# Layer 2 of a four-layer kernel: logits straight from x, and z by token beside the routing

## The chip, the cores and the metric

The kernel runs on one core of one Trainium2 chip. Times are device microseconds (us) of one execution. A core has a matrix engine (TensorE, PE in the views; PEld are its weight loads), a vector engine (VectorE, DVE), an activation engine (ScalarE, ACT), GpSimd (POOL) and a queue engine (SyncE, SP). Each runs its own list of instructions in order, and they wait for one another through semaphores. DMA queues move data between HBM and on-chip memory.

## What is computed

x is (2, 1024, 256), 2048 tokens of 256 numbers. Four layers add to it in turn. Each layer has a conditioning, z = cond(x), and a mixture of experts on z:

```
x = x + ffn0(cond0(x)); x = x + ffn1(cond1(x)); x = x + ffn2(cond2(x)); x = x + ffn3(cond3(x))
```

The change is in layer 2:

```
# cond2: one weight matrix (256 x 256) and one bias per batch row, by category
z = einsum('bti,bio->bto', x, W[cat]) + b[cat][:, None, :]
# ffn2
x_red  = z @ w_red                                  # 256 -> 16
wg_n   = wg / max(norm(wg, axis=1), 1e-4)           # 8 x 16
logits = x_red @ wg_n.T                             # 8 experts
gates  = softmax(logits); score = max(gates); idx = argmax(gates)
h = gelu(z @ W1[idx] + b1[idx])                     # 256 -> 512
o = (h @ W2[idx] + b2[idx]) * score                 # 512 -> 256
```

All of it is in fp32. Every large product is made of three matmuls: each operand is split into a high part (rounded to the engine's fast fp32r format) and a low part, and high x high, high x low and low x high are added up.

## The kernel before

Tokens lie on 128 partitions in NT = 16 tiles; NC = 4 chunks are 4 tiles each (512 tokens); KD = 2 is the number of 128-wide parts of the 256 features. The program is written out by hand: what an engine does next is the order of the code in its block, and semaphores (named `s_...`) tie the engines together. The change touches the seam between layer 1's expert blocks and layer 2's.

**Experts.** Layers 0 to 2 send each token to a block of 256 rows of its expert. `top1` (DVE) makes the softmax; `choose` in it marks the chosen expert; `ranks` (PE) counts tokens per expert with two fp32 matmuls; `order` (DVE) turns the counts into slots and writes one-hot tables (OHH, and OHL in four chunks); `slot_tokens` multiplies them on PE (16 matmuls), and on DVE turns the result into `slot_rows` (TOK), the list of token rows of each block. GpSimd then gathers rows of z from a copy in HBM (`z_rows`, ZD) by indirect DMAs into `w1_raw`, and `blocks` runs over pairs of blocks. GpSimd's first gather waits for slot_rows (`s_tok`) and for the stores of z (`s_zd`). SP's first two weight loads of a layer write over `z_tok` (Z), so that they too wait for `s_zd`.

**The seam before**, engine by engine, line numbers of the code before:
- SP: after layer 1's last block it reads y back from HBM into z_tok, chunk by chunk, then b[cat], spread over the partitions, into w2_raw (the last loop of `block_weights`).
- DVE: splits the conditioning's weights (`cond_split(2)`, L1728), adds y to x (`add_back`, L2050) and makes the low parts of x2's transposes (`lo`, L1717); then adds the bias to each tile of z (L2759), makes the low parts of z2's transposes, finishes the normalising of wg (L2763 to L2767), and starts `top1(2)`.
- PE: transposes x ("x2", L799) into featB; multiplies each token tile of x with W (6 matmuls, L787 to L789), which gives z by token; transposes z ("z2") into featA; multiplies with w_red (24 matmuls, 16 columns of weights); transposes wg_n (L1366); 16 fp32 matmuls for the logits (L1370); ranks(2), slot_tokens(2), blocks(2).
- ACT: the high parts of the transposes (L1389), a copy of x_red (L1694), the square root for the norm (L1696), the exponential (`exps`, L1401).

Layer 1 has no reduction, and takes its logits in another form, which `logits_t` and `logits` write: chunk by chunk the router (8 columns) is the stationary operand and the transposed z moves past it, ACT copies the 8 x 512 result, and 16 small transposes bring it back to tokens on partitions.

## Time and profile before

| | us |
|---|---|
| median of 3 runs | 1270.58 |
| lowest, highest | 1270.04, 1271.40 |
| profiled execution, as a run | 1275.55 |
| its span in the trace | 1273.9 |
| PE busy in the span | 1090.1 (86%) |
| DVE busy | 940.2 (74%) |
| ACT busy | 643.5 (51%) |
| POOL busy | 506.4 (40%) |

Durations in the rows come from the profiled execution, whose span is 1273.9 us; all times of day in the text are us from the span's start. "Idle before, releaser" in brackets behind a row is the time that the engine stood still ahead of it and what let it go; "issue" means that nothing visible held it. [...]

### The profile page before, as it was taken

Reading aid. Unit: us, or ns where it says so; the run is one execution under the profiler, and the core shown is the slowest. Engines: PE = TensorE matmul, PEld = TensorE weight load, DVE = VectorE, ACT = ScalarE, POOL = GpSimd, SP = SyncE. Lnnn points to the kernel's source line nnn. Section 1 sums busy time; section 2 is a strip of 40 time slices with the busy share of each in tenths; the row PEclk is TensorE's granted clock in tenths of the full one; section 3 lists DMA queues with packets and bytes.
Section 4 is the critical chain, followed back from the end, with each engine's and each line's share of the span. In section 5 each row is a group of like instructions: output and inputs, shape, how many; then the busy total and the mean of one; then the engine's idle time right before and its main releaser. Section 6 shows DMA issues by size and latency. Waiting matters only on the chain.

```text
span 1273.9 us, 25855 instructions
## 1 busy us (share of the span) xinstructions
PE 1090.1 (86%) x7884; PEld 1015.1 (80%) x7884; DVE 940.2 (74%) x1622; ACT 643.5 (51%) x1358; POOL 506.4 (40%) x345
## 2 busy tenths in 40 slices
PE   5788958999999999999968739997847976889796
PEld 4577958999999999999965539997737975668685
DVE  6767795888888888888837558884646866767695
ACT  3435316676676677677624537771225734313221
POOL 5000023878888888788730034542006760000000
PEclk8789888999999999999977859998758997989998
DMA  7300326677777778767540156653216844221202
GB/s 184 109 18 3 101 63 245 217 221 250 236 211 253 236 208 254 240 209 244 149 95 1 67 198 240 220 180 103 83 43 214 255 149 157 67 83 35 84 17 67
DMA packets 82030, 191.39 MB, mean 150 GB/s; under 512 B 16819, under 2 KB 57011, under 8 KB 69683
## 3 DMA queue, kind: packets, MB, share of 16 engines
q1 hardware_dynamic: 60050, 150.48, 34.8%
q0 software_dynamic: 21920, 40.21, 13.0%
q8 instruction: 26, 0.43, 0.1%
q14 instruction: 34, 0.27, 0.1%
HBM read 157.48 MB, written 33.18 MB: 150 GB/s over the span
## 4 chain that ended last, share of the span: by engine, by line
PE 68%; DVE 13%; issue 9%; DMA 5%; ACT 2%; DVEq 1%; SPq 1%; POOLq 0%; POOL 0%; ACTq 0%
PE ps L787 22%; PE ps L788 21%; PE ps L789 21%; PE ps L912 2%; DVE hidden_lo L1717 2%; PE ps L799 1%; DMA y_rows<-w_raw,slot_rows 1%; DMA w_raw<-z_rows,slot_rows 1%; DVE featB_lo L1717 1%; DVE x_tok L2050 1%; DVE featA_lo L1717 1%; DMA z_tok<-y_rows 1%; DVE w_lo L1717 1%; DMA z_tok<-in_L_w 1%; DVE z_tok L2446 0%
## 5 line engine op out<-in xcount | busy, mean ns | idle before, releaser
L1458 ACT ACTIVATE hidden_f<-ps,b_block 128x256 f32<-128x256 f32 x432 | 220.6, 511 | 172.4 <-PE ps L789 168.8
L677 POOL DMA_INDIRECT x_tok<-z_gate_rows,slot_rows x76 | 204.7, 2693 | 236.7 <-DVE slot_rows L1884 160.0
L1459 ACT ACTIVATE hidden_hi<-ps,b_block 128x256 fp32r<-128x256 f32 x432 | 222.4, 515 | 0.0
L1717 DVE TENSOR_TENSOR hidden_lo<-hidden_f,hidden_hi 128x512 fp32r<-128x512 f32 x284 | 183.9, 691 | 30.4 <-ACT hidden_hi L1459 16.0
L787 PE MATMUL ps<-w_hi,featA_hi 128*128 128x256 f32 (+1 forms) x624 | 179.4, 288 | 9.2 <-DVE featA_lo L1717 4.0
L787 PE MATMUL ps<-featB_hi,hidden_hi 128*128 128x256 f32 x616 | 175.9, 286 | 3.7 <-DVE hidden_lo L1717 3.7
L789 PE MATMUL ps<-w_hi,featA_lo 128*128 128x256 f32 (+1 forms) x624 | 178.9, 287 | 0.0
L788 PE MATMUL ps<-w_lo,featA_hi 128*128 128x256 f32 (+1 forms) x624 | 178.7, 286 | 0.0
L788 PE MATMUL ps<-featB_lo,hidden_hi 128*128 128x256 f32 x616 | 173.7, 282 | 0.0
L789 PE MATMUL ps<-featB_hi,hidden_lo 128*128 128x256 f32 x616 | 172.5, 280 | 0.0
L705 POOL DMA_INDIRECT x_rows<-w_raw,slot_rows x76 | 130.1, 1712 | 35.4 <-issue 21.9
L677 POOL DMA_INDIRECT w_raw<-z_rows,slot_rows x44 | 57.2, 1300 | 205.2 <-DVE slot_rows L1884 161.6
L787 PEld LDWEIGHTS ps<-w_hi,featA_hi 128*128 128x128 f32 (+1 forms) x624 | 122.0, 195 | 11.0 <-DVE featA_lo L1717 4.7
L788 PEld LDWEIGHTS ps<-w_lo,featA_hi 128*128 128x128 f32 (+1 forms) x624 | 121.8, 195 | 0.0
L789 PEld LDWEIGHTS ps<-w_hi,featA_lo 128*128 128x128 f32 (+1 forms) x624 | 121.8, 195 | 0.0
L787 PEld LDWEIGHTS ps<-featB_hi,hidden_hi 128*128 128x128 f32 x616 | 115.9, 188 | 4.3 <-DVE hidden_lo L1717 4.3
L789 PEld LDWEIGHTS ps<-featB_hi,hidden_lo 128*128 128x128 f32 x616 | 116.4, 189 | 0.0
L788 PEld LDWEIGHTS ps<-featB_lo,hidden_hi 128*128 128x128 f32 x616 | 115.8, 188 | 0.0
L1989 DVE TENSOR_TENSOR w_raw<-ps,b_block 128x256 f32<-128x256 f32 x120 | 49.7, 418 | 63.7 <-PE ps L789 58.0
L787 PE MATMUL ps<-w_hi,featB_hi 128*128 128x256 f32 x288 | 84.7, 294 | 8.7 <-DVE w_lo L1717 5.9
L1717 DVE TENSOR_TENSOR featA_lo<-scratch,featA_hi 128x2048 fp32r<-128x2048 f32 (+3 forms) x47 | 85.5, 1820 | 4.8 <-ACT featA_hi L1576 4.1
L787 PE MATMUL ps<-w_hi,hidden_hi 128*128 128x256 f32 x256 | 76.9, 301 | 8.2 <-DVE hidden_lo L1717 6.0
(446 smaller groups left out, 2969.6 us busy)
## 6 DMA issues: line engine op xcount, KB each, us to landing
scratch<-in_L_w SPq DMA_DIRECT2D x48, 1024.0 KB, 4.9
z_tok<-in_L_w SPq DMA_DIRECT2D x29, 1024.0 KB
x_tok<-in_L_w SPq DMA_DIRECT2D x19, 1024.0 KB, 4.9
b_block<-in_L_ffn_b POOLq DMA_DIRECT2D x60, 128.0 KB
...
```

Of the source, the lines that this page charges most:

```text
L677: gp.indirect_dma_start(XBL[L][:, k, tt, :], None, ZD if L else ZD0, bass.IndirectOffsetOnAxis(ap=TOK[:, q * BTT + tt:q * BTT + tt + 1], a ...
L705: gp.indirect_dma_start(XD, bass.IndirectOffsetOnAxis(ap=TOK[:, q * BTT + tt:q * BTT + tt + 1], axis=0), YB[:, k, tt, :], None, compute_op ...
L787: nc.tensor.matmul(out, lh, rh, start=first, stop=False)
L788: nc.tensor.matmul(out, lh, rl, start=False, stop=False)
L789: return nc.tensor.matmul(out, ll, rh, start=False, stop=last)
L799: last = nc.tensor.transpose(PS[:, g % 4, j * P:(j + 1) * P], src[:, c * TPC + j, k * P:(k + 1) * P], ident[:])
L912: last = nc.tensor.transpose(PS[:, 6 + k, m * BT + tt * P:m * BT + (tt + 1) * P], XBL[L][:, k, tt, m * P:(m + 1) * P], ident[:])
L1458: act.activation(HF[:, f // 2, part], ps, func, bias=b1)
L1459: act.activation(HTh[:, k, f // 2, part], ps, func, bias=b1).then_inc(s_hhi[L], 1)
L1717: return nc.vector.tensor_tensor(out, full, hi.bitcast(F32), ALU.subtract)
L1989: nc.vector.tensor_tensor(YB[:, k, j, :], PS[:, 4 + j, 0:D], B2B[:, k, :], ALU.add).then_inc(s_yev[L], 1)
L2050: nc.vector.scalar_tensor_tensor(X[:, n, :], Z[:, n, :], SM[:, 1, n:n + 1], X[:, n, :], ALU.mult, ALU.add).then_inc(s_add, 1)
```

## The change

With M = w_red @ wg_n.T (256 x 8), logits = (x @ W[cat] + b[cat]) @ M = x @ (W[cat] @ M) + b[cat] @ M. The changed kernel forms K = W[cat] @ M per batch row (256 x 8) and the constant b[cat] @ M, and takes the logits of layer 2 from the transposed x with K as router, in layer 1's form; z is no longer transposed.

- M is formed at the head of layer 1: the norm of wg (DVE, ACT's square root), a transpose and two small fp32 matmuls on PE, ahead of x1's transposes.
- K and the constant are formed between layer 1's blocks and x2's transposes: 8 + 4 fp32 matmuls on PE over the transposed W (WT2, two loads of 256 KB into hidden_f32 after layer 1's last hidden block) and the bias column CB2; DVE splits K and copies the constant.
- z keeps its matmuls by token. Its bias is now added on PE by two matmuls with one row each (a row of ones times the high and the low part of b), and ACT copies each tile to z_tok. Four tiles stand ahead of ranks(2), twelve behind it.
- The one-hot tables of layer 2 move from featB to featA, since featB still holds x.
- SP loads w_red and the bias transposed (the host prepares these and W transposed), two small loads more and one less at the kernel's start.

```diff
@@ SP, after layer 1's blocks
+                if L == 1:
+                    sp.wait_ge(s_hlo[1], steps * LAYERS[1][1] // P)
+                    for b in range(B):
+                        sp.dma_start(WT2[:, b], t["L2_cond_W_t"][bass.ds(cat[b], 1), :, :]
+                                     .rearrange("o (k p) i -> p (o k) i", p=P)).then_inc(s_craw, 16)
+                        sp.dma_start(BROW[:, b * D:(b + 1) * D], t["L2_cond_b"][bass.ds(cat[b], 1), :]).then_inc(s_craw, 16)
@@ PE, logits_t
+                if L in (1, 2):
+                    pe.wait_ge(s_tlo, TR0["z1" if L == 1 else "x2"] + KD * (c + 1))
+                if (L, c) == (2, 0):
+                    pe.wait_ge(s_reds, 3)
@@ PE, head of layer 1
+            pe.wait_ge(s_rstd, NT + 1)
+            nc.tensor.transpose(PS[0:GR, 7, 0:8], WG[:, 2 * GR:3 * GR], ident[0:8, 0:8]).then_inc(s_red, 1)
+            pe.wait_ge(s_reds, 1)
+            for k in range(KD):
+                last = nc.tensor.matmul(PS[:, 7, 16 + 8 * k:24 + 8 * k], WRT[:, k * P:(k + 1) * P], WGT[:], start=True, stop=True)
+            last.then_inc(s_red, 1)
             transposes("x1", X, lambda c: pe.wait_ge(s_x[c], 16 * 2))
@@ PE, the seam
-            transposes("x2", X, tiles_done(1))
-            pe.wait_ge(s_csplit, 3)
-            for n in range(NT):
...
-                last.then_inc(s_cy, 1)
-            transposes("z2", Z, lambda c: pe.wait_ge(s_z0, NT + TPC * (c + 1)))
-            pe.wait_ge(s_tlo, TR0["z2"] + KD * NC)
-
-            for c in range(NC):
-                for k in range(KD):
-                    last = mm3(PS[0:GR, c, :], Rh[2][:, k, :], Rl[2][:, k, :], TAh[:, k, c * CH:(c + 1) * CH],
-                               TAl[:, k, c * CH:(c + 1) * CH], k == 0, k == KD - 1)
-            last.then_inc(s_red, 1)
-            pe.wait_ge(s_rstd, NT + 1)
-            nc.tensor.transpose(PS[0:GR, 5, 0:8], WG[:, 2 * GR:3 * GR], ident[0:8, 0:8]).then_inc(s_red, 1)
-
-            pe.wait_ge(s_reds, 2)
-            for n in range(NT):
-                last = nc.tensor.matmul(PS[:, 4, n * 8:(n + 1) * 8], HF[0:GR, n // TPC, (n % TPC) * P:(n % TPC + 1) * P],
-                                        WGT[:], start=True, stop=True)
-            last.then_inc(s_lg, 1)
+            pe.wait_ge(s_reds, 2)
+            pe.wait_ge(s_craw, CRAW[2])
+            for b in range(B):
+                for m in range(KD):
+                    for k in range(KD):
+                        nc.tensor.matmul(PS[:, 7, m * 16 + b * 8:m * 16 + b * 8 + 8], WT2[:, b, k, m * P:(m + 1) * P], MCR[:, k, :],
+                                         start=k == 0, stop=k == KD - 1)
+                for k in range(KD):
+                    last = nc.tensor.matmul(PS[:, 7, 32 + b * 8:40 + b * 8], CB2[:, b, k:k + 1].broadcast_to([P, P]), MCR[:, k, :],
+                                            start=k == 0, stop=k == KD - 1)
+            last.then_inc(s_red, 1)
+
+            transposes("x2", X, tiles_done(1), lambda c: logits_t(2, c))
+            logits(2)
+
+            def z2(n):
...
+                if n >= 4:
                     pe.wait_ge(s_z0, NT + n - 3)
+                out = PS[:, n % 4, 0:D]
+                row = slice(b * D, (b + 1) * D)
+                nc.tensor.matmul(out, ONEh, BRh[:, row], start=True, stop=False)
+                nc.tensor.matmul(out, ONEh, BRl[:, row], start=False, stop=False)
                 for k in range(KD):
+                    w = slice((b * KD + k) * D, (b * KD + k + 1) * D)
+                    last = mm3(out, TBhv[:, k, n * P:(n + 1) * P], TBlv[:, k, n * P:(n + 1) * P],
+                               W1h[:, 1, w], W1l[:, 1, w], False, k == KD - 1)
                 last.then_inc(s_cy, 1)
+
+            pe.wait_ge(s_csplit, 3)
+            for n in range(TPC):
+                z2(n)
             ranks(2)
+            for n in range(TPC, NT):
+                z2(n)
             slot_tokens(2)
             blocks(2)
@@ ACT
-            transposes("x2", TBhv)
-            transposes("z2", TAh)
-            act.wait_ge(s_red, 1)
-            act.activation(HF[0:GR, :, :], PS[0:GR, 0:4, :], ACT.Copy).then_inc(s_reds, 1)
-            act.wait_ge(s_var, NC + 1)
-            act.activation(SM[0:8, 4, 0:1], SM[0:8, 4, 0:1], ACT.Sqrt).then_inc(s_std, 1)
+            transposes("x2", TBhv, lambda c: logits_t(2, c))
+            for n in range(NT):
+                act.wait_ge(s_cy, NT + n + 1)
+                act.activation(Z[:, n, :], PS[:, n % 4, 0:D], ACT.Copy).then_inc(s_z0, 1)
             exps(2, NT * 8)
@@ DVE, the seam
+            dve.wait_ge(s_craw, CRAW[2])
+            link(nc.vector.tensor_copy(BRh, BROW))
+            lo(BRl, BROW, BRh)
+            link(nc.vector.tensor_copy(ONEh, ONE[0:1, :]))
             cond_split(2, [(P, slice(0, B * KD * D))])
+            dve.wait_ge(s_red, 3)
+            km = PS[:, 7, 0:32].rearrange("p (k e) -> p k e", k=KD)
+            link(nc.vector.tensor_copy(Rh[2][:], km))
+            nc.vector.tensor_copy(CBL, PS[:, 7, 32:48].rearrange("p (b e) -> p b e", b=B))
+            link(lo(Rl[2][:], km, Rh[2][:]))
+            dve.sem_inc(s_reds, 1)
             add_back(1, "x2", TBhv, TBlv)
-            for n in range(NT):
-                dve.wait_ge(s_cy, NT + n + 1)
-                b = n // TPB
-                nc.vector.tensor_tensor(Z[:, n, :], PS[:, 4 + n % 4, 0:D], W2r[:, b * D:(b + 1) * D],
-                                        ALU.add).then_inc(s_z0, 1)
-            transposes("z2", TAh, TAl)
...
             top1(2)
```

PE, between the last matmul of layer 1's blocks and the first of layer 2's conditioning; before:

```order
L950 UNCONDITIONAL_BRANCH
L949 REGISTER_ALU
L949 COMPARE_AND_BRANCH
L799 MATMUL ps<-ident,x_tok 128x128 x32
L787 MATMUL ps<-w_hi,featB_hi 128x256
```

and now (router_raw holds M, hidden_f the transposed W, cond_b the bias column):

```order
L1377 MATMUL ps<-router_raw,hidden_f 128x8 x4
L1380 MATMUL ps<-router_raw,cond_b 128x8 x2
L1377 MATMUL ps<-router_raw,hidden_f 128x8 x4
L1380 MATMUL ps<-router_raw,cond_b 128x8 x2
L814 MATMUL ps<-ident,x_tok 128x128 x16
L802 MATMUL ps<-featB_hi,router_hi 8x512
L803 MATMUL ps<-featB_lo,router_hi 8x512
L804 MATMUL ps<-featB_hi,router_lo 8x512
```

Twelve small fp32 matmuls stand ahead of the transposes, and logits of a chunk follow the transposes of the next one.

PE, from z to the slot tables; before:

```order
L789 MATMUL ps<-featA_hi,router_lo 16x512
L1366 MATMUL ps<-ident,wg 16x8
L1370 MATMUL ps<-wg_t,hidden_f 128x8 x16
L888 MATMUL ps<-scratch,tri 128x128
L889 MATMUL ps<-scratch,ones 128x128
L897 MATMUL ps<-featB_lo,featB_hi 128x32 x16
```

and now, where four z tiles end and the other twelve begin (L1393 and L1394 are the one-row bias matmuls, L907 and L908 the ranks):

```order
L804 MATMUL ps<-w_hi,featB_lo 128x256
L907 MATMUL ps<-scratch,tri 128x128
L908 MATMUL ps<-scratch,ones 128x128
L1393 MATMUL ps<-w_hi 128x256
L1394 MATMUL ps<-w_lo,w_hi 128x256
L802 MATMUL ps<-w_hi,featB_hi 128x256
L803 MATMUL ps<-w_lo,featB_hi 128x256
```

The ranks stand between z tiles, and slot_tokens stands behind all sixteen of them.

DVE, ahead of layer 2's add; before:

```order
L2752 TENSOR_REDUCE small<-wg 8x1
L1728 CAST w_hi<-w_raw 128x1024
L1717 TENSOR_TENSOR w_lo<-w_raw,w_hi 128x1024
L2050 SCALAR_TENSOR_TENSOR x_tok<-z_tok,small,x_tok 128x256 x8
L1717 TENSOR_TENSOR featB_lo<-ps,featB_hi 128x512 x2
```

and now:

```order
L2798 CAST w_hi<-hidden_f 1x512
L1751 TENSOR_TENSOR w_lo<-hidden_f,w_hi 1x512
L2800 CAST w_hi<-ones 1x128
L1762 CAST w_hi<-w_raw 128x1024
L1751 TENSOR_TENSOR w_lo<-w_raw,w_hi 128x1024
L2804 CAST router_hi<-ps 128x32
L2805 COPY router_raw<-ps 128x2x8
L1751 TENSOR_TENSOR router_lo<-ps,router_hi 128x32
L2086 SCALAR_TENSOR_TENSOR x_tok<-z_tok,small,x_tok 128x256 x8
```

The split of the bias row stands ahead of the weights' split, and the three operations on PE's result stand between it and the add.

## Rows read from the trace of the kernel before

**Rows 1.** page, part 4: chain that ended last, by engine.

```profile
PE 68%; DVE 13%; issue 9%; DMA 5%; ACT 2%; DVEq 1%; SPq 1%; POOLq 0%; POOL 0%; ACTq 0%
```

**Rows 2.** stretches: us, busy of each engine (x instructions), granted clock, DMA.

```profile
890.50:903.00 12.50, 10.34 (x50) 9.53 (x51) 10.76 (x23) 4.78 (x8) 0.00 (x0) 0.54 0.24 76
...
912.40:937.50 25.10, 18.66 (x91) 12.88 (x89) 6.21 (x16) 8.96 (x12) 0.00 (x0) 0.77 0.07 24
```

**Rows 3.** chain of waits over the seam: start us, us, what.

```profile
913.02 2.90 DMA z_rows<-z_tok
...
961.14 0.58 PE L787 MATMUL ps<-w_hi,featB_hi 128*128 128x256 f32 x1 [1.41 <-issue]
```

**Rows 4.** timelines of POOL and PE: first gathers, layer 1's first block matmul.

```profile
748.30 1.02 POOL L677 DMA_INDIRECT w_raw<-z_rows,slot_rows  x1 [92.64 <-DVE slot_rows L1884]
...
952.23 0.99 POOL L677 DMA_INDIRECT w_raw<-z_rows,slot_rows  x1 [68.92 <-DVE slot_rows L1884]
...
758.79 0.58 PE L787 MATMUL ps<-w_hi,featB_hi 128*128 128x256 f32 x1 [1.41 <-DVE w_lo L1717]
```

**Rows 5.** timeline of PE: start us, us, engine line op, [idle before <-releaser].

```profile
930.37 6.99 PE L1370 MATMUL ps<-wg_t,hidden_f 16*128 16x8 f32 x32 [0.25 <-DVE wg_t L2767]
```

**Rows 6.** timeline of PE, layer 1: from 128 rows to 16.

```profile
717.04 0.29 PE L1308 MATMUL ps<-featB_hi,hidden_lo 128*128 128x258 f32 x1
717.25 0.38 PE L1314 MATMUL ps<-featA_hi 16*128 16x258 f32 x1
717.48 0.28 PE L1315 MATMUL ps<-featA_lo,featA_hi 16*128 16x258 f32 x1
717.60 0.28 PE L1316 MATMUL ps<-featA_hi,featA_lo 16*128 16x258 f32 x1
```

**Rows 7.** timelines at layer 1's end: PE's last matmul, then DVE.

```profile
881.33 0.28 PE L789 MATMUL ps<-featA_hi,hidden_lo 128*128 128x256 f32 x1
...
883.97 0.16 DVE L2751 TENSOR_TENSOR wg<-wg 8x16 f32<-8x16 f32 x1 [1.89 <-issue]
...
888.83 3.26 DVE L2050 SCALAR_TENSOR_TENSOR x_tok<-z_tok,small,x_tok 128x256 f32<-128x256 f32 x8 [2.65 <-DMA z_tok<-y_rows]
...
900.93 0.69 DVE L1717 TENSOR_TENSOR featB_lo<-ps,featB_hi 128x512 fp32r<-128x512 f32 x1 [0.16 <-ACT featB_hi L1389]
```

**Rows 8.** timelines of PE and ACT, head of layer 1.

```profile
662.01 5.87 PE L799 MATMUL ps<-ident,x_tok 128*128 128x128 f32 x32 [11.85 <-DMA x_tok<-x_rows]
...
669.30 0.69 ACT L1639 ACTIVATE hidden_f<-ps,cond_b 64x512 f32<-64x512 f32 x1 [0.65 <-PE ps L789]
```

**Rows 9.** timelines, layer 1: DVE's last low part, its softmax, ACT's z copies.

```profile
729.45 1.29 DVE L1717 TENSOR_TENSOR featA_lo<-ps,featA_hi 128x512 fp32r<-128x512 f32 x2 [0.97 <-ACT featA_hi L1389]
...
733.53 0.29 DVE L1755 TENSOR_TENSOR scratch<-ps,br 128x128 f32<-128x128 f32 x1 [2.51 <-PE ps L825]
...
719.41 1.57 ACT L1659 ACTIVATE z_tok<-ps,small 128x256 f32<-128x256 f32 x4 [1.72 <-DVE small L2712]
```

**Rows 10.** timeline of PE, layer 1: transposes of z and logits.

```profile
721.03 3.63 PE L799 MATMUL ps<-ident,z_tok 128*128 128x128 f32 x16 [2.07 <-ACT z_tok L1659]
...
724.96 0.40 PE L789 MATMUL ps<-featA_hi,router_lo 128*8 128x512 f32 x1
...
725.89 1.03 PE L799 MATMUL ps<-ident,z_tok 128*128 128x128 f32 x8
```

**Rows 11.** timelines of DVE and PE: routing of layer 2.

```profile
937.47 0.29 DVE L1757 COPY scratch<-ps 128x128 f32<-128x128 f32 x1 [6.86 <-PE ps L1370]
...
939.57 0.80 PE L888 MATMUL ps<-scratch,tri 128*128 128x128 f32 x2 [2.20 <-DVEq L1792]
...
940.82 0.29 DVE L1816 COPY scratch<-ps 128x128 f32<-128x128 f32 x1 [1.37 <-PE ps L889]
...
946.95 2.49 DVE L1845 TENSOR_TENSOR featB_hi<-lane,slot_low 128x512 fp32r<-128x512 int32 x4
...
947.69 3.59 PE L897 MATMUL ps<-featB_lo,featB_hi 128*128 128x32 f32 x16 [6.90 <-DVE featB_hi L1845]
```

More of the change, by code:

```diff
@@ L207, in build @@
         RHT = [[x[:, k, 3, 0:B * P] for x in (HTh, HTl)] for k in range(2)]
+        WRT = W1r[0:GR, 2 * P:2 * P + D]
+        MCR, CBL = Rr[2][:, :, 0:8], Rr[2][:, :, 8:16]
+        WT2 = HF[:, 0:2, :].rearrange("p b (k i) -> p b k i", k=KD)
+        BROW = HF[0:1, 2, :]
+        BRh, BRl, ONEh = W2h[0:1, 0, 0:B * D], W2l[0:1, 0, 0:B * D], W2h[0:1, 1, 0:P]
         CR0 = HF[:, 0:2, :].rearrange("p a c -> p (a c)")
@@ L234, in build @@
         s_craw = sem("cond_raw")
-        CRAW = [16 * n for n in (2 * B, 2 * B + 1, 3 * B + 1, 4 * B + 1)]
+        CRAW = [16 * n for n in (2 * B, 2 * B + 2, 5 * B + 2, 6 * B + 2)]
         s_csplit = sem("cond_split")
@@ L406, in _ @@
             sp.dma_start(B1[0][:], t["L0_b1_t"]).then_inc(s_cb0, 16)
-            for L, name in enumerate(("L0_ffn_Wr", "L1_ffn_Wr", "L2_ffn_w_red", "L3_router_t")):
+            for L, name in ((0, "L0_ffn_Wr"), (1, "L1_ffn_Wr"), (3, "L3_router_t")):
                 sp.dma_start(Rr[L][:], t[name].rearrange("(k p) e -> p k e", p=P)).then_inc(s_small, 16)
@@ L553, in block_weights @@
                                  ).then_inc(s_x[c], 16)
-                if L == 1:
-                    for b in range(B):
-                        sp.dma_start(W2r[:, b * D:(b + 1) * D], t["L2_cond_b"][bass.ds(cat[b], 1), :]
-                                     .broadcast_to([P, D])).then_inc(s_rows, 16)
             for L in SPARSE:
@@ L896, in slot_tokens @@
                         pe.wait_ge(s_inv, 15 + (1 + NC) * (L - 1) + n // TPC + 2)
-                    last = nc.tensor.matmul(PS[:, 5, 16 * NT:16 * NT + SCOLS[L]], OHL[:, n, :], OHH[:, n, :],
+                    last = nc.tensor.matmul(PS[:, 5, 16 * NT:16 * NT + SCOLS[L]], OHL[L][:, n, :], OHH[L][:, n, :],
                                             start=n == 0, stop=n == NT - 1)
@@ L1395, in logits_t @@
             def logits_t(L, c):
+                E = 8 if L == 2 else RW[L]
                 act.wait_ge(s_lt, LT0[L] + c + 1)
-                act.activation(LT[0:RW[L], c, :], PS[0:RW[L], 5 + c % 3, :], ACT.Copy).then_inc(s_lts, 1)
+                act.activation(LT[0:E, c, :], PS[0:E, 5 + c % 3, :], ACT.Copy).then_inc(s_lts, 1)
             def exps(L, n):
@@ L1633, in _ @@
             blocks(0)
+            act.wait_ge(s_var, NC + 1)
+            act.activation(SM[0:8, 4, 0:1], SM[0:8, 4, 0:1], ACT.Sqrt).then_inc(s_std, 1)
             transposes("x1", TAh)
@@ L1756, in softmax @@
                 else:
-                    link(nc.vector.tensor_copy(lg, ps))
+                    bte = "p (b t) e -> p b t e"
+                    link(nc.vector.tensor_tensor(lg.rearrange(bte, b=B), ps.rearrange(bte, b=B),
+                                                 CBL.unsqueeze(2).broadcast_to([P, B, TPB, E]), ALU.add))
                 link(nc.vector.tensor_reduce(SM[:, 5, :], lg, axis=AX.X, op=ALU.max))
@@ L2556, in _ @@
             next(masks)
-            for n in range(1, 4):
+            for n in (1, 3):
                 router_split(n)
```

58 lines of the change are left out of this document (31 added, 27 removed).

## The prediction

> **What bounds the kernel now.** The chain of waits comes first: PE holds 68% of it [rows 1], nearly all of that in the expert blocks. The change touches none of the expert blocks, only the seam between layer 1's last block and layer 2's first. So the second view is the table of stretches over that seam [rows 2]. [...] The seam is thus one serial chain: x added up and transposed, z made (903.0 to 912.4), z transposed, reduced and turned into logits (912.4 to 937.5, 25.1 us), routing (to 952), gather (to 961.1). Before the block can start, the list of rows (slot_rows) and the stored z rows must both be there. The chain shows that the last z tile's store runs from 913.02 to 915.9, after which nobody waits for a store; the gather starts at 952.23 and the block's first matmul at 961.14 [rows 3, 4]. Today routing is last, by 36 us. The reader should keep two clocks in mind below: when the rows are listed, and when z is stored.
>
> **Ahead of the add (+0.2 us).** PE gets 12 small fp32 matmuls in front of x2's transposes and DVE waits for them before its add. An fp32 matmul is two instructions in this trace (32 for the 16 of L1370), so 24. Their pace is bounded by two rows: L1370's 32 in 6.99 us at half clock (0.218 each), and 0.12 from start to start, the pace of full-clock matmuls [rows 5, 6]: 2.9 to 5.2 us. PE's last block matmul ends at 881.6; DVE needed 1.9 us to leave the same loop [rows 7], and I take the same for PE: 883.5 to between 886.4 and 888.7. DVE's own chain is 883.97, 1.3 us for the three bias splits, 2.0 for the weight split and some 0.7 for the three new copies: 888.0 to 889.4. The add starts at 888.83 today because y lands then [rows 7]. I take 889.0: +0.2, between 0 and +0.6. The transposed weights (512 KB) are loaded once the last hidden block is split, around 872, and have 11 us; nobody waits for them. The square root and the normalised gate weights move to the head of layer 1, where PE waits 11.9 us for x; I cost them nothing, but they leave another activation table loaded, and the reload (1.28 us) comes just before tanh, where ACT has 0.65 us free [rows 8]. That is +0.6, between 0 and 1.3.
>
> **Logits from x (32.9 us earlier).** Layer 1 already does what layer 2 now will: from its last featA_lo (ends 730.74) to softmax's first operation (733.53) are 2.8 us [rows 9]. Layer 2's last featB_lo ends at 901.6 [rows 7], +0.2 = 901.8, so softmax starts at 904.6 instead of 937.47. PE must keep pace for that. Per chunk it has six logit matmuls at 0.23 us and eight transposes in about 1.0 (four logit starts from 724.96 to 725.89, then 1.03) [rows 10], 2.4 us against DVE's 2.9 (four adds, two splits), at full clock. What goes away (z's 32 transposes, the 24 reductions, their copies, the Sqrt chain and the 7 us of L1370) needs no price, since the sum is built forward.
>
> **z on PE (the term that decides).** PE keeps its order: four z tiles, the rank matmuls, twelve z tiles, then slot_tokens. A tile is 6 matmuls at 0.12 us plus two with one row for the bias: 8 x 0.119 = 0.95. But the one-row pair needs the array with another number of rows. Where the trace switches from 128 rows to 16, the starts are 717.04, 717.25, 717.48, 717.60: two gaps of 0.21 and 0.23 where 0.12 is the pace, 0.20 lost for a switch [rows 6]. Each tile switches twice: 0.95 + 0.39 = 1.34 us; the bounds are 0.95 and 1.34, and I take 1.34, the nearest row. [...]
>
> Tiles 0 to 3: 904.4 + 5.4 = 909.8. Without them the ranks would start 2.1 us after softmax (939.57 against 937.47), at 906.7, so 3.1 us of the gain are given back. Ranks take 1.25 us at half clock [rows 11]; I take 0.7 at full clock. DVE's ordering then runs from 910.5 for 8.6 us (940.82 to 949.44) to 919.1 [rows 11]. PE's other twelve tiles: 910.4 + 12 x 1.34 = 926.5. PE, not DVE, is last, by 7.4 us. Two things follow from tile 15. slot_tokens: 16 matmuls, 1.9 us at full clock (3.59 at half [rows 11]), and DVE's three operations, 0.8: the rows are listed at 929.2. z: ACT's copy 0.45 (four in 1.57 in layer 1 [rows 9]), store 2.9 [rows 3]: 930.05. So **z's store becomes the last wait** in place of the list, and the gather starts at 930.3 instead of 952.23. ACT's exponential stands behind all 16 copies, with its table load: 928.8, just ahead of where DVE asks for it; nothing.
>
> **Gather and weights.** Gather to first matmul is 8.9 us in layer 2 (952.23 to 961.14) and 10.5 in layer 1 (748.30 to 758.79), where two weight loads of 1 MB follow the gather [rows 3, 4]. In the changed kernel the first-weight loads write over z and so also wait for the store: 4 x 512 KB leave with the gather, as many bytes as in layer 1. I take 10.5 (bounds 8.9 and 13). First block matmul: 940.8 against 961.14, a gain of 20.3; less 0.6 in layer 1, **19.7 us**. The clock that the block starts with (0.50) is the same, since PE idles some 10 us before it in both. From there on nothing moves. The profiled execution took 1275.55 us for a span of 1273.9; the span becomes 1254.2, and the median, 1270.58, becomes **1250.9, say 1251**.
>
> **Rivals.** [...] (B) PE runs the x2 stage at half clock. Today the stretch 890.5 to 903.0 stands at 0.54 [rows 2]. Layer 1's transposes begin at half clock too, and the clock is back after 3.4 us of unbroken work [rows 10]; here the first 16 transposes and the first logits join likewise, but later chunks leave gaps. At half clock a chunk takes 6 x 0.43 + 1.97 = 4.5 us against DVE's 2.9, some 5 us over the stage, up to 3 more on the first z tiles: 1256 to 1259, say 1257. (C) Gathers queue behind 2 MB of weights that today have long landed: 3 to 5 us more, 1255. (D) Slower than before: the engine falls to half clock in the stage and stays there as it did from 930 to 937, with PE busy throughout [rows 5]. The seam would still be 5 us shorter (z tiles 34 us instead of 21), but each us of block work costs another 0.8; from 6 us of blocks at half clock on beyond what they have now, the gain is gone, and 12 us of it give 1275. Against it: every block so far reaches 1.00 within 6 us. (E) The bias by PE makes DVE free, but z is not hidden beside routing, only partly: that is in the forecast, not apart.
>
> **How the numbers follow.** Forecast 0.52 (its own range 1247 to 1254: the store or gather some 3 us off), A 0.20, B 0.18, C 0.08, D 0.02. The predicted time is the likeliest case's, 1251. The range goes from A's 1243 to B's 1258 and leaves out less than 2 in 10. A measurement of this kernel tells about 0.2% (2.5 us) from no change: faster 0.96; same 0.02, for B and C together with a gather that is worse still; slower 0.02.
>
> **What would show it.** In the changed profile: softmax's first operation of layer 2 near 904.6 (B: 909 or later); starts of the z tiles 1.34 us apart (A: 0.95), with gaps at the one-row pair; slot_tokens following tile 15 at once, and DVE idle some 7 us before it; the gather released by the z store and not by slot_rows, near 930; first block matmul 10.5 us behind it. The forecast is wrong if the routing, and not z's store, is again last, if the add of layer 2 starts later than 889.5, or if the clock of the stretch from 895 to 926 is below 0.9.

## The result and the profile after

The changed kernel takes 1264.6 us (median of ten runs, 1254.5 to 1268.1) where the kernel before takes 1271.3 (ten runs, 1266.1 to 1274.6). The ratio is 0.9941, 95% interval 0.9916 to 0.9967: faster, but by 0.6% only. That is 6.7 us from median to median where 19.6 were forecast, and 6.6 us above the upper end of the range. The profiled execution has a span of 1264.9 us (before: 1273.9). Two executions far longer than the rest of their kernels (2701.4 us of the kernel before, 1295.8 us of the one below with pairs in tiles 0 to 7) are left out of all medians and ratios.

The chain that ended last has the same shape as [rows 1]. First the page of the changed kernel, part 4:

```profile
PE 68%; DVE 13%; DMA 7%; issue 6%; ACT 2%; POOL 1%; POOLq 1%; SPq 1%; DVEq 0%; ACTq 0%
```

The stretches of the changed kernel that answer to [rows 2] (us, busy time of PE, weight load, DVE, ACT, POOL with their instructions, granted clock, DMA share, GB/s):

```profile
886.90:894.00 7.10, 5.34 (x22) 4.05 (x23) 6.65 (x15) 2.39 (x4) 0.00 (x0) 0.54 0.59 189
894.00:901.50 7.50, 7.39 (x51) 4.06 (x50) 5.05 (x12) 4.29 (x8) 0.00 (x0) 1.00 0.00 0
901.50:904.30 2.80, 2.80 (x20) 2.40 (x18) 1.81 (x6) 0.38 (x1) 0.00 (x0) 0.90 0.03 6
904.30:909.00 4.70, 4.70 (x18) 3.80 (x18) 0.00 (x0) 0.77 (x2) 0.00 (x0) 0.50 0.00 0
...
930.00:937.00 7.00, 7.00 (x26) 5.66 (x26) 0.00 (x0) 1.15 (x3) 0.00 (x0) 0.50 0.21 70
```

Read the clock column, the number behind POOL's: the granted clock as a share of full clock, 1.00 full and 0.50 half. While x is transposed and the logits are made, the clock comes up to 1.00, at 893.5. In the z tiles it stands at 0.50 from 903.7 to their end at 937.5, 33.8 us in which PE is busy throughout. The timeline of PE shows where it fell (L1393 and L1394 are the one-row bias matmuls, L802 to L804 the products of full height; start, duration in us):

```profile
901.57 0.36 PE L1393 MATMUL ps<-w_hi 1*128 1x256 f32 x1
901.77 0.28 PE L1394 MATMUL ps<-w_lo,w_hi 1*128 1x256 f32 x1
901.97 0.39 PE L802 MATMUL ps<-w_hi,featB_hi 128*128 128x256 f32 x1
...
902.89 0.38 PE L1393 MATMUL ps<-w_hi 1*128 1x256 f32 x1
...
903.54 0.28 PE L803 MATMUL ps<-w_lo,featB_hi 128*128 128x256 f32 x1
903.65 0.34 PE L804 MATMUL ps<-w_hi,featB_lo 128*128 128x256 f32 x1
903.79 0.42 PE L802 MATMUL ps<-w_hi,featB_hi 128*128 128x256 f32 x1
904.01 0.42 PE L803 MATMUL ps<-w_lo,featB_hi 128*128 128x256 f32 x1
...
904.57 0.58 PE L1393 MATMUL ps<-w_hi 1*128 1x256 f32 x1
...
906.87 0.58 PE L1393 MATMUL ps<-w_hi 1*128 1x256 f32 x1
```

Tile 0 takes 1.32 us (901.57 to 902.89), as forecast for full clock. In the middle of tile 1, at 903.7, the step from matmul to matmul goes from 0.12 to 0.21 us, and PE is not idle anywhere near. From tile 2 on each tile takes 2.30 us. Sixteen tiles and the ranks (1.05 us) last from 901.57 to 937.49, 35.9 us, where 16 x 1.34 + 0.7 = 22.1 had been counted.

What waits for it, on the timelines of DVE and POOL, and then PE's first work of the block (these answer to [rows 3, 4, 7 and 11]):

```profile
886.93 3.25 DVE L2086 SCALAR_TENSOR_TENSOR x_tok<-z_tok,small,x_tok 128x256 f32<-128x256 f32 x8 [0.99 <-DMA z_tok<-y_rows]
901.82 0.29 DVE L1792 TENSOR_TENSOR scratch<-ps,router_raw 128x128 f32<-128x128 f32 x1 [2.52 <-PE ps L844]
910.13 0.29 DVE L1852 COPY scratch<-ps 128x128 f32<-128x128 f32 x1 [6.33 <-PE ps L908]
940.96 0.19 DVE L1916 TENSOR_SCALAR scratch<-ps 128x32 f32<-128x32 f32 x1 [22.20 <-PE ps L916]
```

```profile
941.88 0.99 POOL L692 DMA_INDIRECT w_raw<-z_rows,slot_rows  x1 [60.50 <-DVE slot_rows L1920]
```

```profile
937.49 3.43 PE L916 MATMUL ps<-featA_lo,featA_hi 128*128 128x32 f32 x16
950.31 1.11 PE L931 MATMUL ps<-ident,w_raw 128*128 128x128 f32 x4 [9.38 <-DMA w_raw<-z_rows,slot_rows]
952.83 0.58 PE L802 MATMUL ps<-w_hi,featB_hi 128*128 128x256 f32 x1 [1.41 <-DVE w_lo L1751]
```

The span is 9.0 us shorter. Of that, 1.9 us are there by the add (886.93, before 888.83 [rows 7]). The seam, add to first block matmul, is 65.9 us against 72.3, a gain of 6.4 where 20.5 were forecast. The rest, first block matmul to the end of the span, is 312.1 against 312.8.

### The profile page after: what moved, and what is told of

The parts are those of the page before. It is cut to its first block, busy times and chain, and to the rows that moved or that the text cites. A ratio compares the mean times of both kernels' runs of the same rounds, so it can differ in the third digit from the quotient of the medians.

```text
span 1264.9 us, 25881 instructions
## 1 busy us (share of the span) xinstructions
PE 1103.9 (87%) x7896; PEld 1021.3 (81%) x7896; DVE 930.8 (74%) x1603; ACT 647.0 (51%) x1370; POOL 506.3 (40%) x345
## 4 chain that ended last, share of the span: by engine, by line
PE 68%; DVE 13%; DMA 7%; issue 6%; ACT 2%; POOL 1%; POOLq 1%; SPq 1%; DVEq 0%; ACTq 0%
PE ps L802 21%; PE ps L803 21%; PE ps L804 20%; DMA y_rows<-w_raw,slot_rows 2%; PE ps L931 2%; DVE hidden_lo L1751 2%; DMA w_raw<-z_rows,slot_rows 1%; DMA z_tok<-in_L_w 1%; PE ps L814 1%; DVE featB_lo L1751 1%; DVE x_tok L2086 1%; DVE featA_lo L1751 1%; DMA z_tok<-y_rows 1%; PE ps L1393 1%; DMA x_rows<-w_raw,slot_rows 1%
## 5 line engine op out<-in xcount | busy, mean ns | idle before, releaser
L692 POOL DMA_INDIRECT x_tok<-z_gate_rows,slot_rows x76 | 208.8, 2748 | 233.1 <-DVE slot_rows L1920 158.7
L802 PE MATMUL ps<-w_hi,featA_hi 128*128 128x256 f32 (+1 forms) x624 | 179.1, 287 | 8.4 <-ACT hidden_hi L1493 3.9
L802 PE MATMUL ps<-featB_hi,hidden_hi 128*128 128x256 f32 x616 | 176.0, 286 | 3.4 <-DVE hidden_lo L1751 3.4
L804 PE MATMUL ps<-w_hi,featA_lo 128*128 128x256 f32 (+1 forms) x624 | 178.1, 285 | 0.0
L804 PE MATMUL ps<-featB_hi,hidden_lo 128*128 128x256 f32 x616 | 172.8, 280 | 0.0
L720 POOL DMA_INDIRECT x_rows<-w_raw,slot_rows x76 | 126.7, 1668 | 35.7 <-issue 21.9
L802 PEld LDWEIGHTS ps<-w_hi,featA_hi 128*128 128x128 f32 (+1 forms) x624 | 121.2, 194 | 10.5 <-DVE featA_lo L1751 4.1
L804 PEld LDWEIGHTS ps<-w_hi,featA_lo 128*128 128x128 f32 (+1 forms) x624 | 121.2, 194 | 0.0
L802 PEld LDWEIGHTS ps<-featB_hi,hidden_hi 128*128 128x128 f32 x616 | 116.3, 189 | 3.9 <-DVE hidden_lo L1751 3.8
L804 PEld LDWEIGHTS ps<-featB_hi,hidden_lo 128*128 128x128 f32 x616 | 116.5, 189 | 0.0
L802 PE MATMUL ps<-w_hi,featB_hi 128*128 128x256 f32 x288 | 90.5, 314 | 7.2 <-DVE w_lo L1751 6.0
L803 PE MATMUL ps<-w_lo,featB_hi 128*128 128x256 f32 x288 | 86.7, 301 | 0.0
```

The lines of the kernel that those rows point to most:

```text
L692: gp.indirect_dma_start(XBL[L][:, k, tt, :], None, ZD if L else ZD0, bass.IndirectOffsetOnAxis(ap=TOK[:, q * BTT + tt:q * BTT + tt + 1], a ...
L720: gp.indirect_dma_start(XD, bass.IndirectOffsetOnAxis(ap=TOK[:, q * BTT + tt:q * BTT + tt + 1], axis=0), YB[:, k, tt, :], None, compute_op ...
L802: nc.tensor.matmul(out, lh, rh, start=first, stop=False)
L803: nc.tensor.matmul(out, lh, rl, start=False, stop=False)
L804: return nc.tensor.matmul(out, ll, rh, start=False, stop=last)
```

## The experiments

Each run has a mean clock, the granted clock averaged over its whole span; only one run of each kernel, the profiled one, has a trace that shows where the clock stood. H1 says that the pair of one-row matmuls ahead of each z tile lets the clock fall. H2, the rival, says that the clock falls whatever the tiles hold, because of the sparser work just ahead (transposes, logits of 8 columns). H3 says that something else takes the time. The seam is compared from trace to trace as the time from the add to the block's first matmul: 72.3 us before, 65.9 after.

### Without the bias

```diff
-                nc.tensor.matmul(out, ONEh, BRh[:, row], start=True, stop=False)
-                nc.tensor.matmul(out, ONEh, BRl[:, row], start=False, stop=False)
...
-                               W1h[:, 1, w], W1l[:, 1, w], False, k == KD - 1)
+                               W1h[:, 1, w], W1l[:, 1, w], k == 0, k == KD - 1)
```

> The changed kernel without the two one-row bias matmuls of each z tile (z comes out without its bias, so this part of the computation is left out). Theory H1, the one-row pair with its two changes of row count is what lets the clock fall: each tile is then six matmuls of 0.119 us = 0.72 us at granted clock 1.00, the stage behind the softmax is bound by the ordering on DVE (about 914), and the first gather comes some 22 us earlier than the 941.9 of the changed kernel: about 1242 us, ratio to before 0.977. Rival H2, the clock falls whatever the tiles are made of, because of the sparse stretch of transposes and 8-column logits ahead of them: tiles of 6 x 0.214 = 1.28 us, stage 20.5 us, gather at about 928, about 1251 us. Rival H3, the tiles need nothing from the clock and the time is lost elsewhere: no change from 1264.

Measured: 1242.2 us (four runs, 1238.4 to 1245.2), ratio 0.9775 (0.9742 to 0.9807). Its stretches and POOL's first gather:

```profile
901.50:904.30 2.80, 2.80 (x30) 2.78 (x30) 1.72 (x6) 1.04 (x3) 0.00 (x0) 1.00 0.02 6
904.30:909.00 4.70, 4.70 (x42) 4.70 (x42) 2.96 (x15) 2.28 (x7) 0.00 (x0) 1.00 0.33 112
```

```profile
918.51 0.99 POOL L692 DMA_INDIRECT w_raw<-z_rows,slot_rows  x1 [36.51 <-DMA z_rows<-z_tok]
```

The clock stays at 1.00 behind exactly the same transposes and logits, so H2 in its plain form falls, and H3 with it. It goes down only at 917.9, when PE has finished z and the product of the slot tables. The seam is 41.0 us.

### The same bias over 128 rows

```diff
-        BROW = HF[0:1, 2, :]
-        BRh, BRl, ONEh = W2h[0:1, 0, 0:B * D], W2l[0:1, 0, 0:B * D], W2h[0:1, 1, 0:P]
+        BROW = HF[:, 2, :]
+        BRh, BRl, ONEh = W2h[:, 0, 0:B * D], W2l[:, 0, 0:B * D], W2h[:, 1, 0:P]
...
-            link(nc.vector.tensor_copy(ONEh, ONE[0:1, :]))
+            link(nc.vector.tensor_scalar(ONEh, ident[:], 0.0, 1.0 / P, ALU.mult, ALU.add))
```

The load of the bias row is broadcast to all partitions as well.

> The changed kernel with the bias matmuls made over 128 rows instead of one: the bias row copied to all 128 partitions, the ones row replaced by a 128x128 tile of 1/128. No change of row count is left, everything is computed. H1 (the one-row pair is the cause): 8 x 0.119 = 0.95 us a tile at granted clock 1.00, 16 tiles and the ranks 16 us from 901.6, z tile 15 done at 917.5, DVE's order at 914.5 to 918, gather at about 922: about 1245 us, ratio 0.980. H2 (the stretch ahead is the cause): 8 x 0.214 = 1.71 us a tile, 27.4 us, gather at about 935, about 1257 us, ratio 0.989.

Measured: 1245.1 us (five runs, 1243.4 to 1248.9), ratio 0.9804 (0.9779 to 0.9829). Two stretches, and the gather:

```profile
904.30:909.00 4.70, 4.70 (x42) 4.70 (x42) 2.30 (x12) 1.70 (x5) 0.00 (x0) 1.00 0.33 112
...
914.00:919.00 5.00, 5.00 (x46) 5.00 (x44) 1.05 (x2) 2.65 (x6) 0.00 (x0) 1.00 0.32 108
```

```profile
921.98 0.99 POOL L693 DMA_INDIRECT w_raw<-z_rows,slot_rows  x1 [40.21 <-DMA z_rows<-z_tok]
```

This is H1 as a remedy: as many matmuls of as many columns as in the changed kernel, everything computed, and the seam is 45.3 us in place of 65.9. By the forecast's own price, 6 us of the 20.6 are the changes of row count (16 x 0.39), and the rest is the clock.

### The pairs of four tiles together

```diff
+            def bias4(n):
+                if n:
+                    pe.wait_ge(s_z0, NT + n)
...
+                for j in range(4):
+                    nc.tensor.matmul(PS[:, j, 0:D], ONEh, BRh[:, row], start=True, stop=False)
+                    nc.tensor.matmul(PS[:, j, 0:D], ONEh, BRl[:, row], start=False, stop=False)
```

> The changed kernel with the bias matmuls of four tiles made together ahead of the four tiles: as many one-row matmuls as before, but 8 changes of row count instead of 32. If the one-row matmuls themselves pull the clock down: granted 0.50, 8 x 0.214 = 1.71 us a tile plus a few gaps, 28 us for the stage in place of 36, about 1257 us. If the gaps at the changes of row count do it: clock 1.00, about 1.05 us a tile, 17 us, about 1246 us. If neither (H2): 0.50 and 28 us as in the first case, so this run parts gaps from the rest only if the clock stays up.

Measured: 1248.9 us (four runs, 1246.2 to 1249.7), ratio 0.9818 (0.9791 to 0.9845).

```profile
901.50:904.30 2.80, 2.80 (x21) 2.67 (x20) 1.81 (x6) 0.00 (x0) 0.00 (x0) 0.73 0.03 6
904.30:909.00 4.70, 4.67 (x31) 4.40 (x30) 0.98 (x4) 1.53 (x4) 0.00 (x0) 0.80 0.03 10
909.00:914.00 5.00, 4.53 (x35) 4.13 (x34) 4.55 (x19) 1.54 (x4) 0.00 (x0) 1.00 0.38 128
```

Neither case as written. The clock fell behind the first eight one-row matmuls, which follow the logits, came back 3.4 us later (902.8 to 906.2) in the 24 full matmuls, and did not fall again behind the other three groups. So the one-row matmuls can bring it down, but not everywhere.

### The pair in the kernel before

```diff
+                    if k == 0:
+                        for j in range(2):
+                            nc.tensor.matmul(PS[:, 4 + n % 4, 0:D], ONEh, W2h[0:1, 0, 0:D], start=j == 0, stop=False)
...
-                               W1h[:, 1, w], W1l[:, 1, w], k == 0, k == KD - 1)
+                               W1h[:, 1, w], W1l[:, 1, w], False, k == KD - 1)
```

> The kernel before, with two one-row matmuls (a row of ones by a row of zeros, so they add nothing) put ahead of each z tile; its z tiles stand behind 128-column transposes as before and ran at granted clock 1.00 from 902. H1: the clock falls to 0.50 inside the z tiles, tiles of 2.30 us from then on, the stage some 20 to 25 us longer, about 1293 us. H2 (it takes the logits stretch ahead): the clock stays 1.00, tiles of 1.32 us, the stage 16 x 0.6 = 10 us longer, about 1281 us.

Measured: 1295.3 us (two runs, 1291.6 and 1298.9), ratio 1.0189 (1.0147 to 1.0231). Stretches of this kernel:

```profile
895.00:903.00 8.00, 7.19 (x28) 5.79 (x28) 5.49 (x11) 2.39 (x4) 0.00 (x0) 0.50 0.00 0
...
930.00:937.00 7.00, 7.00 (x28) 6.04 (x28) 1.27 (x3) 0.00 (x0) 0.00 (x0) 0.50 0.01 2
937.00:945.00 8.00, 6.19 (x37) 4.67 (x36) 5.06 (x8) 4.46 (x8) 0.00 (x0) 0.88 0.20 66
```

In the kernel before, the clock rises to 1.00 at 902, early in the z tiles, which follow each other at 0.72 us from then on. With the pair it never rises while the tiles last (899.5 to 936.1), and does so at 938.9, in the transposes behind them. Thirty-two matmuls that add zero cost 24 us, some 10 of which are what they and their changes of row count last at full clock (0.6 us a tile, an estimate from the expectation above). So the pairs' effect on the clock is there without anything else that the change does, and without 8-column logits ahead. But it is another half of the effect: here the pairs kept at 0.50 a clock that stood there already, and in the changed kernel they let one fall.

### Rows, switches, or their number

Three kernels ask what it is about the pair. A pair over 64 rows (the 128-row diff with 64 in place of P):

> The bias pair of each z tile made over 64 rows instead of one (64 rows of 1/64, the bias row on 64 partitions): as many matmuls and as many changes of row count as in the changed kernel, but 64 rows at work. If the changes of row count and their gaps hold the clock down: granted 0.50 from about 904, 2.3 us a tile, about 1264 us as the changed kernel. If it is the one-row work: clock 1.00 and 0.95 + 0.39 = 1.34 us a tile, 22 us for the stage, about 1251 us; or, should a change from 128 rows to 64 cost nothing, 0.95 us a tile and about 1245 us as with 128 rows.

Only one of the two one-row matmuls:

```diff
-                nc.tensor.matmul(out, ONEh, BRl[:, row], start=False, stop=False)
```

> The changed kernel with only one of the two one-row matmuls in each z tile (the low part of the bias is left out): as many changes of row count, half the one-row work. If the changes of row count hold the clock down: granted 0.50, about 2.30 - 0.21 = 2.09 us a tile, 3 us less than the changed kernel, about 1261 us. If the amount of one-row work decides: the clock stays up, 7 x 0.119 + 0.39 = 1.22 us a tile, gather at about 926, about 1249 us.

And the kernel with 128 rows with a small matmul that changes the row count and does next to nothing:

```diff
+                nc.tensor.matmul(PS[:, n % 4, D:D + 8], ONEh[0:1, :], BRh[0:1, 0:8], start=True, stop=True)
                 nc.tensor.matmul(out, ONEh, BRh[:, row], start=True, stop=False)
```

> The kernel with 128-row bias matmuls (1245 us, clock 1.00 through the z tiles), plus, ahead of each tile, one more matmul of one row and 8 columns into unused columns of the same bank: it brings back the two changes of row count a tile and next to no one-row work. If the changes of row count and their gaps let the clock fall: granted 0.50 for most of the z tiles, 1.71 + 0.7 = 2.4 us a tile, up to 1268 us. If it takes the one-row matmuls of 256 columns: the clock stays 1.00, 0.95 + 0.39 = 1.34 us a tile, about 1251 us.

Measured: 64 rows 1254.8 us (four runs, 1250.3 to 1265.6), ratio 0.9866 (0.9830 to 0.9903); one matmul 1253.1 (1247.6 to 1255.1), 0.9853 (0.9815 to 0.9891); changes of row count alone 1250.6 (1249.3 to 1252.7), 0.9835 (0.9812 to 0.9857). The last one first, stretches of the z tiles:

```profile
904.30:909.00 4.70, 4.70 (x35) 4.25 (x35) 0.97 (x3) 1.15 (x3) 0.00 (x0) 1.00 0.00 0
...
919.00:924.00 5.00, 5.00 (x35) 4.52 (x35) 0.00 (x0) 1.54 (x4) 0.00 (x0) 1.00 0.33 108
```

The clock stays at 1.00 and the kernel costs 5.5 us more than the one with 128 rows, 0.34 a tile: the two changes of row count, for which 0.39 was forecast. So the gaps at the changes cost what they last and did not bring the clock down here. With 64 rows the profiled run (1265.6 us, mean clock 0.911) fell like the changed kernel, in its second tile, and the gap at the switch is there too:

```profile
903.65 0.38 PE L1394 MATMUL ps<-w_hi 64*128 64x256 f32 x1
903.87 0.28 PE L1395 MATMUL ps<-w_lo,w_hi 64*128 64x256 f32 x1
...
905.64 0.33 PE L804 MATMUL ps<-w_lo,featB_hi 128*128 128x256 f32 x1
...
906.75 0.58 PE L1394 MATMUL ps<-w_hi 64*128 64x256 f32 x1
```

The other three took 1250.3 to 1256.3 at mean clocks of 0.919 to 0.926, near the 1251 of a clock that stays up; without a trace of them that is a hint and no proof. With one matmul per tile the clock fell at 905.3, in the second tile too, and was back by 912.1 while the one-row matmuls went on. That is neither of the two cases expected (1261 and 1249):

```profile
904.30:909.00 4.70, 4.70 (x20) 3.59 (x19) 1.03 (x4) 1.15 (x3) 0.00 (x0) 0.61 0.01 3
909.00:914.00 5.00, 5.00 (x24) 4.14 (x23) 2.78 (x14) 0.85 (x3) 0.00 (x0) 0.68 0.31 105
914.00:919.00 5.00, 5.00 (x30) 3.82 (x29) 4.76 (x13) 1.65 (x5) 0.00 (x0) 1.00 0.27 92
```

Fewer such matmuls made the low stretch shorter, and taller ones let the clock fall just the same in the one run that has a trace. So it is no property of one-row matmuls alone.

### Where the pairs stand

Four kernels start from the one with 128 rows and use the one-row pair in some tiles only. They differ from one another in the condition (here for pairs from tile 8 on):

```diff
+                q = slice(0, P if n < NT // 2 else 1)
+                one = ONEh if n < NT // 2 else ROW1
+                nc.tensor.matmul(out, one[q], BRh[q, row], start=True, stop=False)
+                nc.tensor.matmul(out, one[q], BRl[q, row], start=False, stop=False)
```

> Bias over 128 rows in z tiles 0 to 7 and by the one-row pair in tiles 8 to 15, so that the pairs begin deep in dense work at full clock. If the pairs pull the clock down whatever stands ahead: it falls to 0.50 a few us behind tile 8, tiles of 2.30 us, z done at about 927 in place of 917.7, about 1254 us. If they only keep it down, or do so only with the sparse stretch of transposes and logits right ahead: 1.00 to the end, 1.34 us a tile, z done at 921, about 1248 us.

> The one-row pair in z tiles 0 to 3 alone, right behind the logits, and the 128-row bias in tiles 4 to 15. If the pairs make the clock fall and hold it: it falls to 0.50 near 904, as in the changed kernel, and comes back within a few us behind tile 4, as it came back in the kernel with grouped bias; about 1250 us. If a clock that fell there stays down whatever follows: tiles of 1.71 us to the end, z done near 929, about 1257 us. If four pairs don't make it fall: 1.00 throughout, about 1247 us.

> The 128-row bias in z tiles 0 to 3, the one-row pair in tiles 4 to 15. Twelve pairs in a row behind 3.8 us of dense tiles; eight behind dense tiles (0 to 7) kept the clock at 1.00. If a long run of pairs lets the clock fall wherever it begins: 0.50 from some tile on, each tile from there 2.30 us in place of 1.34; with the fall at tile 8, 8 us more than the 1249.5 us that twelve pairs at full clock would give, about 1257 us. If the pairs do it only right behind the transposes and logits: 1.00 to the end, about 1249.5 us (1245 + 12 x 0.39).

> The one-row pair in z tiles 0 to 7, right behind the logits, the 128-row bias in tiles 8 to 15. Four such pairs left the clock at 1.00 in the profiled run, sixteen brought it to 0.50 from 903.7 on. If it takes pairs right behind the transposes and logits: the clock falls in a part of the runs and comes back within a few us behind tile 8, 1248 us in runs without a fall (1245 + 8 x 0.39), up to 1256 us in runs with one. If the fall needs more pairs than eight: all runs near 1248 us.

| pairs in tiles | clock in the z tiles, profiled run | runs, us | ratio (95%) |
|---|---|---|---|
| 8 to 15 | 1.00 throughout | 1248.1 (4 runs, 1247.1 to 1250.3) | 0.9826 (0.9792 to 0.9860) |
| 4 to 15 | 1.00 throughout | 1250.5 (6 runs, 1248.7 to 1252.4) | 0.9820 (0.9795 to 0.9846) |
| 0 to 3 | 1.00 throughout | 1246.7 (4 runs, 1244.8 to 1247.4) | 0.9798 (0.9776 to 0.9819) |
| 0 to 7 | 0.50 from tile 1 (902.2), back in tile 8 (919.2) | 1254.2 (5 runs, 1246.5 to 1258.4) | 0.9844 (0.9807 to 0.9881) |

Pairs in tiles 4 to 15, the late part of the z tiles:

```profile
909.00:914.00 5.00, 5.00 (x31) 3.92 (x31) 4.52 (x20) 1.53 (x4) 0.00 (x0) 1.00 0.30 103
914.00:919.00 5.00, 5.00 (x32) 3.93 (x30) 2.68 (x5) 1.46 (x4) 0.00 (x0) 1.00 0.31 105
```

Pairs in tiles 0 to 7:

```profile
901.50:904.30 2.80, 2.80 (x12) 2.21 (x13) 0.77 (x3) 0.77 (x2) 0.00 (x0) 0.62 0.00 0
...
914.00:919.00 5.00, 5.00 (x21) 4.55 (x22) 3.31 (x6) 0.77 (x2) 0.00 (x0) 0.50 0.00 0
919.00:924.00 5.00, 5.00 (x43) 5.00 (x43) 0.00 (x0) 1.92 (x5) 0.00 (x0) 0.97 0.37 124
```

PE of this kernel where the clock fell (L1397 is the first matmul of tile 1's pair), and then a stretch of the kernel with pairs in tiles 0 to 3:

```profile
901.42 0.38 PE L1397 MATMUL ps<-w_hi 1*128 1x256 f32 x1
...
902.38 0.42 PE L804 MATMUL ps<-w_hi,featB_hi 128*128 128x256 f32 x1
```

```profile
904.30:909.00 4.70, 4.70 (x33) 4.02 (x34) 1.01 (x3) 1.47 (x4) 0.00 (x0) 1.00 0.00 0
```

Twelve pairs behind four dense tiles: no fall, and all six times lie within 3 us of the 1249.5 of a full clock. Eight pairs right behind the logits: a fall in the profiled run, and the clock back as soon as dense tiles follow. The times of its five runs spread from 1246.5 to 1258.4, where 1248 was expected without a fall; the kernel with 128 rows alone spreads over 5.5 us, so they hint at falls in some runs and none in others, but don't show it.

The last two lines of the table must not be read as "eight pairs bring the clock down and four don't". The clock fell at 902.2, in tile 1, when two pairs had run, and in the changed kernel too two had run at 903.7. Up to tile 3 the kernels with pairs in tiles 0 to 3 and 0 to 7 are the same on PE, and in the one profiled run of the first the clock did not fall. So the same work, in the same order, can go either way. One thing differed from trace to trace, the moment: the first pair ran 8.1 us behind the last rise of the clock in the changed kernel, 8.2 us in the one with pairs in tiles 0 to 7, and 8.9 us in the one with pairs in tiles 0 to 3 (but 9.2 us where the eight one-row matmuls of four tiles stood together, and there it fell). No run varied this by itself, and none changed what stands ahead of the pairs (x's transposes, the logits, and the sixteen transposes of 8 rows and 8 columns behind them).

What the traces show is therefore this: every fall in the z tiles came where pairs, or their like, stood right behind that stretch, and with pairs from tile 4 or 8 on there was none. H2 seems to be half of the truth, for the fall; to keep a low clock low, the pairs were enough in the kernel before.

### Two kernels that beat both

One bias matmul of 128 rows, the high part on rows 0 to 63 and the low part on rows 64 to 127:

```diff
-            lo(BRl, BROW, BRh)
+            link(nc.vector.tensor_tensor(BRh[P // 2:P], BROW[P // 2:P], BRh[P // 2:P], ALU.subtract))
...
                 nc.tensor.matmul(out, ONEh, BRh[:, row], start=True, stop=False)
-                nc.tensor.matmul(out, ONEh, BRl[:, row], start=False, stop=False)
```

> One bias matmul of 128 rows in place of two: rows 0 to 63 carry the high part of the bias, rows 64 to 127 the low part, the other operand is 1/64 throughout; everything is computed. PE: 7 x 0.119 = 0.83 us a tile, z done at 915.8 in place of 917.7, DVE's order (8.6 us behind ranks that end 0.5 us earlier) at 914.6, the last store and so the gather 1.9 us earlier than with two bias matmuls, at about 920: about 1243 us, ratio 0.979. If DVE's order were the bound by now: gather at 921 and 1244 us.

Measured: 1242.8 us (five runs, 1241.7 to 1244.1), ratio 0.9776 (0.9758 to 0.9793), as expected. The low part in rows 64 to 127 is the bias less its rounded value, and the other operand is 1/64. The seam is 42.8 us, and the z store is the last wait:

```profile
918.68 0.99 POOL L693 DMA_INDIRECT w_raw<-z_rows,slot_rows  x1 [38.50 <-DMA z_rows<-z_tok]
```

And no bias on PE, but added by POOL, for which the stores of z now wait:

```diff
+                    gp.wait_ge(s_craw, CRAW[2])
+                    for n in range(NT):
+                        gp.wait_ge(s_z0, NT + n + 1)
+                        gp.tensor_tensor(Z[:, n, :], Z[:, n, :], BROW[:, n // TPB * D:(n // TPB + 1) * D], ALU.add).then_inc(s_xb2, 1)
```

> No bias on PE at all; POOL, idle for 60 us there, adds the bias row (held on 128 partitions) to each z tile behind ACT's copy, everything is computed. PE tiles of 0.72 us at full clock end at about 913, POOL's 16 adds at 0.76 us (its add of the same size at the start of the kernel took 12.12 us for 16) end at about 915.5, the last store lands 2.9 us later, gather at 918.5: 3.5 us before the kernel with 128-row bias matmuls, about 1241.5 us, ratio 0.9775. If POOL's adds and DVE's ordering slow each other: adds of 1.2 us or more, z ready at 922 or later, about 1247 us.

Measured: 1243.6 us (six runs, 1239.3 to 1248.7), ratio 0.9798 (0.9765 to 0.9831). POOL kept its pace (0.81 us an add, 0.76 expected), but DVE's ordering, beside it, did not. POOL's timeline, then DVE's:

```profile
906.33 9.68 POOL L768 TENSOR_TENSOR z_tok<-z_tok,hidden_f 128x256 f32<-128x256 f32 x12 [0.27 <-ACT z_tok L1734]
920.91 0.99 POOL L693 DMA_INDIRECT w_raw<-z_rows,slot_rows  x1 [4.90 <-DVE slot_rows L1924]
```

```profile
905.15 0.29 DVE L1856 COPY scratch<-ps 128x128 f32<-128x128 f32 x1 [1.08 <-PE ps L914]
906.37 0.72 DVE L1861 TENSOR_SCALAR scratch<-iota_f 128x8 f32<-128x8 f32 x1
...
915.35 3.01 DVE L1885 TENSOR_TENSOR featA_hi<-lane,slot_low 128x512 fp32r<-128x512 int32 x4
```

The order runs from 905.15 to 918.4, 13.2 us, against 8.6 with POOL idle, and slot_rows, not the store, releases the gather. DVE's operations grew longer beside POOL's adds (0.72 us for the 128x8 operation at 906.37, 0.17 in the changed kernel at 910.91); what the two contend for, the trace doesn't show. What POOL saved on PE it took from DVE.

## Why the prediction was wrong, step by step

**Ahead of the add.** Forecast 889.0, measured 886.93. The 24 small matmuls run from 879.95 to 882.8 on the timeline, at the full-clock bound of 2.9 us, and PE left its loop after 0.27 us, not 1.9; they wait for nobody and nobody waits for them. The lead of 1.9 us is older than the seam: the x transposes at the head of layer 1 start at 659.55, before at 662.01 [rows 8]. It may be mere spread, since over the traces of the other changed kernels, whose code ahead of the add is nearly the same, the add starts anywhere from 885.5 to 889.0. From those transposes to the first featB_lo on DVE, 9.97 us went by (659.55 to 669.52) in place of 8.95 (662.01 to 670.96): the table reload (1.28 us at 666.56) costs 1.0, where 0.6 had been counted within 0 to 1.3.

**Logits from x.** Forecast: softmax 15.6 us behind the add. Measured: 14.9 (886.93 to 901.82), with the clock at 1.00 from 894 on. Right, and rival B, half clock in this stretch, did not come to pass.

**z on PE: the step that failed.** Behind the sentence "A tile is 6 matmuls at 0.12 us plus two with one row for the bias" stood 1.34 us a tile. The switches were priced rightly (1.32 for tile 0; 0.34 a tile in the run with switches alone). What failed is the clock that was taken for them: all sixteen tiles were counted at full clock. From tile 2 on they took 2.30 us, and tiles and ranks took 35.9 us instead of 22.1. Those 13.8 us are the miss, since the seam came out 14.1 us longer than forecast (65.9 against 51.8). With bias matmuls of 128 rows, and little else changed, it is 20.6 us shorter. By the runs, it is the one-row pairs that let the clock fall and held it at 0.50. The profile of before held a warning: in [rows 5] PE is busy for 6.99 us with matmuls over 16 rows, and the clock, down at 929.3 after a stretch in which PE mostly idled, stays at 0.50 (stretch of the kernel before):

```profile
930.00:937.00 7.00, 6.75 (x32) 6.66 (x33) 0.37 (x3) 0.57 (x1) 0.00 (x0) 0.50 0.00 0
```

Against it I had put the places where the clock had come back in unbroken work, such as the transposes of [rows 10], begun at 0.50 at 721.03 and followed by 1.00 from 724.5 on. But there that work was over 128 rows throughout, and here two matmuls in eight are not.

**Rival D** had the mechanism ("falls to half clock in the stage and stays there", z tiles of 34 us, a seam 5 us shorter; measured 34.9 without the ranks, and 6.4) and got 0.02, since I gave it 12 us of slow blocks on top and made it the slower case. The blocks reached full clock as before, 5.5 us behind the first block matmul (958.3; before 5.7, at 966.8), and the rest of the span took 312.1 us against 312.8. Without that addition its time would have been some 1266 (1270.6 less 5), and the range would have had to reach it. D named no cause in the bias matmuls, though, but only that such a stretch had been seen. **Rival A** gave 1244, which is also what the lower end of the range, 1243, rests on: one-row pairs whose changes of row count cost nothing, tiles of 0.95 us. No run shows that term; in the traces a change of row count cost 0.17 to 0.20 us. The kernel with 128 rows, whose tiles take 0.95 because no row count changes in them, took 1245.1.

**What is last.** PE before DVE: right, DVE stood idle for 22.2 us ahead of the list. The z store as the last wait: here the list and the store came together (slot_tokens at half clock took 3.43 us instead of 1.9). With the clock up, the gather is released by the store in the kernels without bias, with 128 rows and with one 128-row matmul, as forecast. (The recorded sum for the store, 926.5 + 0.45 + 2.9, gives 929.85 and not 930.05; that is 0.2 us.)

**Gather to first matmul.** 10.5 forecast, 10.95 measured (941.88 to 952.83); 10.0 to 10.4 in the kernels without bias and with 128 rows. Rival C, 3 to 5 us more here, did not come to pass.
